# Mixer and expert block on one Trainium2 core: the second norm and the store of the result moved one group later, loads issued in the order in which tiles come free, transposed Y in another bank

## The reference, cut to what matters

```python
def reference(x, ...):                      # x: (8, 1024, 128), fp32
    x = _layernorm(x + mixer(x))            # "first norm": gives Y
    x = _layernorm(x + experts(x))          # "second norm": gives the result
    return x

def mixer(x):                               # mLSTM: up projection, causal conv, q, k, v, gates
    ...
    h = (C / norm) @ v                      # C = q k^T * exp(decay - max), causal, 4 heads
    hn = normalise(h per head)
    return ((hn * norm_w + skip * x_act) * silu(z)) @ W_down

def experts(x):                             # 16 experts of width 64, top 4 of 16, plus a shared one
    g = sigmoid(x @ gate_w.T)
    combine = top-4 of g, divided by their sum
    h = silu(x @ e_win) * (x @ e_vin) * combine
    return silu(x @ ws_in) * (x @ vs_in) @ ws_out + h @ e_wout
```

## Time and profile before

| | us |
|---|---|
| median of 3 runs | 912.57 (912.12 to 923.52) |
| the profiled execution | 916.93 |
| its span in the trace | 915.2 |
| second phase, from the first y1 to the last | 698.1 |

### The profile page before, as it was taken

How to read it: one execution, slowest core, us unless ns; L and a number is a source line. 1 busy time by engine, 2 the same in 40 slices (tenths; PEclk the granted TensorE clock), 3 DMA queues, 4 the chain that set the end, 5 groups by cost and what they waited for, 6 DMA issues and landing times.

```text
span 915.2 us, 17726 instructions
## 1 busy us (share of the span) xinstructions
PE 823.2 (90%) x5783; PEld 643.9 (70%) x5783; DVE 669.4 (73%) x1759; ACT 363.3 (40%) x621; POOL 372.1 (41%) x372
## 2 busy tenths in 40 slices
PE   6879866799999999899989999999999999999966
PEld 5646655677777777777777777777777777777754
DVE  5899944577777777777786878777867777878654
ACT  4767742224343434333333443333434343433131
POOL 5040037253536262626262626353726353534200
PEclk8999977699999999999999999999999999999979
DMA  4877734300403040404030403040304040400000
GB/s 114 258 242 271 272 116 119 115 25 24 126 23 126 24 126 23 126 23 126 23 126 23 126 23 126 23 126 23 126 23 126 23 126 23 126 23 24 1 11 12
DMA packets 53104, 81.01 MB, mean 89 GB/s; under 512 B 10176, under 2 KB 36952, under 8 KB 49112
## 3 DMA queue, kind: packets, MB, share of 16 engines
q1 hardware_dynamic: 53080, 80.68, 28.2%
HBM read 55.24 MB, written 25.43 MB: 88 GB/s over the span
## 4 chain that ended last, share of the span: by engine, by line
PE 49%; DVE 17%; issue 14%; DMA 10%; POOL 5%; SPq 3%; ACT 2%; POOLq 1%; DVEq 0%; ACTq 0%
PE bank L1402 12%; DMA max_b<-max_scratch 7%; PE bank L1372 5%; PE bank L1376 5%; PE bank L1373 5%; PE bank L1392 4%; PE bank L1345 3%; DVE st L991 3%; PE bank L1321 3%; DVE acc L839 2%; PE bank L1319 2%; DVE Y L1003 2%; PE bank L1326 2%; DMA x_in<-in_L_attn_x_dram 2%; DVE out_sb L1003 2%
## 5 line engine op out<-in xcount | busy, mean ns | idle before, releaser
L755 ACT ACTIVATE s_in<-bank 128x512 f32<-128x512 f32 x144 | 85.9, 597 | 195.9 <-PE bank L1376 195.0
L1402 PE MATMUL bank<-ewout,h 128*128 128x128 f32 x1024 | 146.5, 286 | 0.0
L1402 PEld LDWEIGHTS bank<-ewout,h 128*128 128x128 f32 x1024 | 123.9, 191 | 25.4 <-issue 25.4
L554 POOL TENSOR_TENSOR rs<-ve,half 128x4 f32<-128x4 f32 x32 | 32.6, 1019 | 267.5 <-DVE ve L999 267.5
L1103 DVE TENSOR_TENSOR h<-s_in,bank 128x512 f32<-128x512 f32 x144 | 98.1, 681 | 58.5 <-PE bank L1376 50.3
L1372 PE MATMUL bank<-yT_hi,in_hi 128*128 128x512 f32 x288 | 128.2, 445 | 6.8 <-DVE h L1103 6.8
L1376 PE MATMUL bank<-yT_lo,in_hi 128*128 128x512 f32 x288 | 115.3, 400 | 0.0
L1373 PE MATMUL bank<-yT_hi,in_lo 128*128 128x512 f32 x288 | 114.6, 398 | 0.0
L540 POOL TENSOR_TENSOR D<-a_tok,max_b 128x512 f32<-128x512 f32 x64 | 65.4, 1043 | 118.5 <-DVE max_b L911 67.9
L1107 DVE TENSOR_TENSOR h<-h,bank 128x512 f32<-128x512 f32 x128 | 87.3, 682 | 19.8 <-PE bank L1392 19.8
L952 DVE TENSOR_TENSOR state<-kept,bank 64x130 f32<-64x130 f32 x128 | 36.6, 286 | 64.8 <-POOL kept L569 34.7
(11 more groups left out here) (197 smaller groups left out, 1634.2 us busy)
## 6 DMA issues: line engine op xcount, KB each, us to landing
xact_scratch<-xact SPq DMA_DIRECT2D x16, 1024.0 KB, 4.9
max_b<-max_scratch SPq DMA_DIRECT2D x15, 1024.0 KB, 7.7
xa<-xact_scratch SPq DMA_DIRECT2D x16, 512.0 KB, 6.4
silu_z<-xact_scratch SPq DMA_DIRECT2D x16, 512.0 KB, 3.8
inter_w<-inter_scratch SPq DMA_DIRECT2D x30, 256.0 KB, 7.0
x_in<-in_L_attn_x_dram SPq DMA_DIRECT2D x16, 256.0 KB, 4.9
xt_scratch<-x_t SPq DMA_DIRECT2D x16, 256.0 KB, 4.8
xT<-xt_scratch SPq DMA_DIRECT2D x16, 256.0 KB, 8.0
```

The costliest lines, as they stand in the source:

```text
L755: act.activation(s_in[:, j % 2], bank[4][:], ACT.Silu).then_inc(silu_done, 1)
L1402: i = pe.matmul(bank[7][:, k * P:(k + 1) * P], h2[:, j % 2, k * P:(k + 1) * P], w, start=(j == k == 0), stop=(j == NJ), skip_group_check=True)
```

## The change

Four things are moved; no arithmetic is added or removed.

1. The statistics of the second norm of group f and the norm itself leave the end of `mix(f + 1)`. In `mix(g, f)` VectorE now does `ffn_statistics(f - 1)` behind slot 2 and `ffn_norm(f - 1)` behind slot 4. Only the sum z2 stays where it was.
2. GpSimd's inverse root rs2 moves with them: from behind rs1 to behind the loop over the four chunks, for group f - 1. Between rs1 and qs nothing is left.
3. SyncE stores the result of group f - 1 behind the load of xa, and then loads max_b for group g + 2 (it waits for the four subtractions of `args(g + 1)` to be done). Before, max_b for g + 1 was loaded at the start of `mix(g)`, behind the store of the group before and x_res.
4. The transposed Y goes to bank 5 and no longer to bank 7, so the waits for z2 move from `ffn_head` to the first output matmul, and waits for h1 and h2 of the group before are added.

The first two and the last two groups stand outside the hardware loop now.

```diff
             mix(0, None)
-            with eng.Fori(1, NG - 1) as g:
+            mix(1, 0)
+            with eng.Fori(2, NG - 2) as g:
                 mix(g, g - 1)
+            mix(NG - 2, NG - 3)
             mix(NG - 1, NG - 2)
             ffn(NG - 1)
...
             def mix(g, f):
-                sp.wait_ge(arg_sub, nth(g, 4, 3))
-                if not (isinstance(g, int) and g == NG - 1):
-                    load_max(g + 1)
+                if not is_last(g):
                     sp.wait_ge(val_mm[1], g + 1)
                     sp.dma_start(xT2[:], xt_d[g + 1]).then_inc(xT_in, 16)
                     sp.wait_ge(qs_done, g + 1)
...
                     load_xa(g + 1)
+                if f is not None and before(f) is not None:
+                    store(before(f))
+                if not is_last(g, 2):
+                    sp.wait_ge(arg_sub, nth(g + 1, 4, 3))
+                    load_max(g + 2)
+                if not is_last(g):
                     for p in range(NP):
                         sp.wait_ge(hs_done[p], g + 1)
                     load_z(g + 1)
-                if f is not None:
-                    store(f)
-                if not (isinstance(g, int) and g == NG - 1):
                     sp.wait_ge(y1_done, g + 1)
                     sp.dma_start(x_res[:], x_g[g + 1]).then_inc(x_res_in, 16)
...
+                if f is not None and before(f) is not None:
+                    norm_power(before(f))
                 for kp in range(2):
...
                 pool.wait_ge(ve1_done, g + 1)
                 power(rs1[:], ve1[:], rs1_done)
-                if f is not None:
-                    ffn(f)
                 if not (isinstance(g, int) and g == NG - 1):
                     weigh_queries(g + 1)
...
             def ffn_head(f):
                 act.wait_ge(yT_mm, f + 1)
-                prev2(act, z2_done, f)
-                copy(yT[:], bank[7][:]).then_inc(yT_out, 1)
-                copy(yT_hi[:], bank[7][:]).then_inc(yT_hi_done, 1)
+                copy(yT[:], bank[5][:]).then_inc(yT_out, 1)
+                copy(yT_hi[:], bank[5][:]).then_inc(yT_hi_done, 1)
...
             def mixer_norm(g):
                 dve.wait_ge(rs1_done, g + 1)
+                prev(dve, z2_done, g)
                 normalise(Y, y1, mv1, rs1, Y_done)
...
                 for j in range(NJ + 2):
                     if f is not None:
                         ffn_slot(f, j)
+                    if f is not None and before(f) is not None:
+                        if j == 2:
+                            ffn_statistics(before(f))
+                        elif j == 4:
+                            ffn_norm(before(f))
...
                 yT_low(g)
-                if f is not None:
-                    ffn_norm(f)
...
             def ffn_sum(f):
                 dve.wait_ge(o_mm, f + 1)
+                prev(dve, out_done, f)
                 dve.tensor_tensor(flat(z2), bank[7][:], flat(Y), ALU.add).then_inc(z2_done, 1)
-                dve.wait_ge(z2_done, f + 2)
+
+            def ffn_statistics(f):
+                dve.wait_ge(z2_done, f + 1)
                 statistics(f, z2, st2, mv2, ve2, st2_done, mv2_done, ve2_done)
...
             def ffn_head(f):
                 pe.wait_ge(Y_done, f + 1)
-                prev2(pe, z2_done, f)
+                prev(pe, h1_done, f, NJ + 1)
                 for k in range(NC):
-                    i = pe.transpose(bank[7][:, k * P:(k + 1) * P], Y[:, k], ident[:])
+                    i = pe.transpose(bank[5][:, k * P:(k + 1) * P], Y[:, k], ident[:])
                 i.then_inc(yT_mm, 1)
 
             def ffn_logits(f):
                 pe.wait_ge(yT_out, f + 1)
+                prev(pe, h2_done, f, NJ)
```

More of the change, by code:

```diff
@@ L323, in groups, with before, is_last @@
             mix(0, None)
-            with eng.Fori(1, NG - 1) as g:
+            mix(1, 0)
+            with eng.Fori(2, NG - 2) as g:
                 mix(g, g - 1)
+            mix(NG - 2, NG - 3)
             mix(NG - 1, NG - 2)
             ffn(NG - 1)
+        def before(f):
+            return None if isinstance(f, int) and f == 0 else f - 1
+        def is_last(g, n=1):
+            return isinstance(g, int) and g >= NG - n
         def prev(eng, s, g, per=1):
@@ L333, in prev @@
             eng.wait_ge(s, g * per)
-        def prev2(eng, s, f):
-            eng.wait_ge(s, f + 1)
         @block.sync
@@ L476, in store, with ffn @@
                 sp.dma_start(out_g[f], out_sb[:]).then_inc(out_stored, 16)
-            groups(sp, mix, store)
+            sp.wait_ge(arg_sub, 4)
+            load_max(1)
+            def ffn(f):
+                store(f - 1)
+                store(f)
+            groups(sp, mix, ffn)
             sp.wait_ge(out_stored, 16 * NG)
@@ L590, in mix, with norm_power, ffn @@
                 power(rs1[:], ve1[:], rs1_done)
-                if f is not None:
-                    ffn(f)
                 if not (isinstance(g, int) and g == NG - 1):
                     weigh_queries(g + 1)
-            def ffn(f):
+            def norm_power(f):
                 pool.wait_ge(ve2_done, f + 1)
                 power(rs2[:], ve2[:], rs2_done)
+            def ffn(f):
+                norm_power(f - 1)
+                norm_power(f)
             pool.memset(state[:], 0.0).then_inc(phase2_const, 1)
@@ L915, in _ @@
             back(2, floor_tok)
-            dve.sem_inc(z2_done, 1)
             all_tok = lambda t: t[:].rearrange("p b f k h -> p (b f) (k h)")
@@ L1041, in mix @@
                 yT_low(g)
-                if f is not None:
-                    ffn_norm(f)
             def yT_low(f):
                 dve.wait_ge(yT_hi_done, f + 1)
-                dve.tensor_tensor(yT_lo[:], bank[7][:], yT_hi[:].bitcast(F32), ALU.subtract).then_inc(yT_lo_done, 1)
+                dve.tensor_tensor(yT_lo[:], bank[5][:], yT_hi[:].bitcast(F32), ALU.subtract).then_inc(yT_lo_done, 1)
             def routing(f, part):
@@ L1128, in ffn @@
                         routing(f, 3)
+                    elif j == 2:
+                        ffn_statistics(f - 1)
+                    elif j == 4:
+                        ffn_norm(f - 1)
                 ffn_sum(f)
+                ffn_statistics(f)
                 ffn_norm(f)
@@ L1398, in ffn_out @@
                     pe.wait_ge(h1_done, nth(f, NJ + 1, 0))
+                    prev(pe, z2_done, f)
                 w = ewout[:, j - 1] if j else wsout[:]
```

## The result

| | before | after |
|---|---|---|
| median, us | 918.01 (4 runs, 912.12 to 923.52) | 983.74 (4 runs, 982.05 to 985.92) |
| profiled execution, us | 916.93 | 985.23 |
| span, us | 915.2 | 983.2 |
| group, second to fifteenth y1, 13 intervals, us | 46.32 | 51.18 |

The ratio after to before is 1.072, with a 95% interval of 1.062 to 1.081: 7% slower. The table has one run of the kernel before more than the prediction had. The ratios given there are against those runs, so the 912.57 from which the prediction started was low.

What follows compares the result with a forecast made beforehand. TensorE's work plus its waits was taken to bound each group. Two blockings gave +26.9 us and clock falls +17.4, together 44.3 on 916.93, or 961.2; the median lies 4.4 lower, so 957 us, range 930 to 988.

Steps and rivals of the forecast that it cites:

- the two blockings: GpSimd's bulk instructions block VectorE at Y behind qs and routing behind D; +26.9 us together with the clock full.
- the first case: Both blockings, with falls of the clock in some groups: 946 to 985 us, forecast 957, chance 0.47.
- the clock down nearly always: Rival: the clock falls behind both waits in most groups, 26.9 + 38 us and more, over 978; chance 0.05.
- What bounds the kernel, and what the change removes: TensorE's work plus waits set the group, 46.32 us; waits from late max_b and the norm on VectorE's path go.
- neither blocking: Rival: neither blocking comes back, a group is 44.14 us and the time 882 us; chance 0.06.
- Y behind qs: VectorE's four Y instructions wait for GpSimd, taking 3.85 us; TensorE gets Y 1.72 later, chunk 1 comes 0.92 later.
- The rule of the Trainium skill: VectorE and GpSimd share a port pair, whole instructions block; by it the sum would be some 1 us x 13 more.
- Routing behind D: Routing part 3's five small VectorE instructions each sit out a GpSimd instruction; +2.29 us from chunk 1 to next y1.
- The clock, +17.4: TensorE's new waits bring half clock in six of 13 groups, 2.9 us each; bounds 0 and 38 us.
- The moved work at nothing: Second norm's statistics behind slot 2 and norm behind slot 4 on VectorE cost 0; upper bound 14 us.
- Banks, other loads: nothing: New waits on banks 5, 6 and 7 cost 0; earlier xT2, inter_w and x_res loads bring no cost or gain.
- The last group, -1.0: No qs follows rs1 there, so Y is free 1.0 us earlier and TensorE, waiting 4.77, gains it.

Runs made afterwards that it cites:

- Early max_b with D held: Kernel before with only max_b loaded early, loop unrolled, and GpSimd starting D only after the routing weights are written: 903.42 us, 0.980 of the kernel before.
- both waits held: Changed kernel with GpSimd waiting for Y before qs and for the routing weights before D: 883.12 us, 0.960 of the kernel before.
- Y's blocking alone: Changed kernel with D held behind the routing weights and 8 unused identity matmuls before TensorE's wait for Y: 916.44 us, 0.995 of the kernel before.
- the filled waits: Changed kernel with unused identity matmuls before TensorE's waits for Y and the routing weights: 956.26 us with 12 in each, 949.26 with 8.
- the run with the spare one: Changed kernel with D held behind the routing weights and an unused inverse root between rs1 and qs on GpSimd: 885.20 us, 0.962 of the kernel before.

## Why the prediction was right, point by point

The sign, the two blockings and their places were right, and 983.74 lies in the range of 930 to 988. It lies close to the range's end, though, and the forecast of 957 was 27 us short. By the number it is still in the first case (946 to 985, falls in some groups). By what happened it is closer to the last (the clock down nearly always, over 978), which had a chance of 0.05. That the range held was in part luck. Where the 27 us are:

| us | in the sum | measured, by spans and y1 |
|---|---|---|
| first phase and first interval | 0 | +3.1 |
| 13 intervals, second to fifteenth y1 | +27.0 + 17.4 | +63.3 |
| interval to the last y1 | +0.9 | +2.2 |
| behind the last y1 | -1.0 | -0.6 |
| median against the profiled execution | -4.4 | -1.5 |

So 19 us are missing in the 13 groups, most of them in the clock's term. Of the other 8, two lie in front of the first y1, which comes anywhere from 165.6 to 176.8 us in the runs here, and three are the low median from which the prediction started.

- **What bounds the kernel, and what the change removes.** Right. Early max_b with D held gained 14 us, and the norm out of the way 1.05 us a group. With neither blocking the prediction had 44.14 a group and 882 us; measured 44.25 and 883.12. That the total agrees so well is in part luck: it started from a low median, and the first interval, which it left as it was, gave 6.7 us (50.50 to 43.78). That max_b would be issued some 20 us before a group ends was off, without effect: in the group shown it is issued at 568.15, 13 us before the end, and D never waited for it.
- **Y behind qs, 3.85 us and TensorE 1.72 later.** Right: 3.86, and the transposes of Y come 537.95 - 530.40 = 7.55 behind y1 instead of 5.64, 1.9 later. Two tenths are missing from the term: 0.1 because rs1 started 2.52 behind y1 (2.41 in the first group), the rest between the end of Y and the transposes. From 12.54 to 14.51 the prediction made 1.97 a group of it; from y1 to chunk 1 it is 12.61 with both waits held and 14.77 with Y's blocking alone, and the groups give 46.43 - 44.25 = 2.2.
- **The rule of the Trainium skill** ("SBUF — State Buffer", section "SBUF: two separate sides") that the whole instruction blocks would have added 1 us more a group. Y's 3.86 us in every group, shorter than qs, `kept` and the skip product together (2.35 + 0.62 + 1.57), is against it for the skip product. For qs and `kept` the trace agrees: the first two instructions of Y take 2.36 and 0.66 us.
- **Routing behind D, +2.29.** Right where the clock is full: 48.71 - 46.43 = 2.28, and from chunk 1 to the next y1 33.9 us with routing blocked and 31.6 without, as forecast (33.89 and 31.60). In the changed kernel itself the wait was 2.08, not 2.5, and chunk 1 to y1 33.4: some of the time that the half clock cost was given back there.
- **The sum without the clock**, 48.40 a group, measured 48.71: 0.3 short, nearly all of it in Y's term.
- **The clock, +17.4: the term that was mis-sized.** "I take a fall in six of the 13 groups" was wrong: it fell in all 13, and twice in two of them. (51.18 - 48.71) x 13 = 32 us, against 17.4; with the 0.3 a group of the line above it is 36. The price of one fall was about right: chunk 1 comes 17.74 us behind y1 instead of 14.8, 2.9 later, of which 0.5 comes back behind it. The prediction also had the place wrong. It laid the falls behind the second wait, as the longer one, from a row where 2.32 us of idling was followed by a fall and 2.07 was not. In the changed kernel the wait for Y, 2.16 us, brought the clock down each time, and the one for the weights in two groups of 13 only (there 2.50 and 2.13). The bound of a fall in each group, 38 us, was the nearer value. Nothing in the rows of the kernel before could tell six falls from 13, and the choice near the middle was a guess.
- **The moved work at nothing.** Right: the statistics fit in front of the third state update (0.3 us of idle left), and no new wait stands in slots 2 to 6.
- **Banks, other loads: nothing.** Right for the banks (1.000). The other loads and the store were not moved alone. No wait of TensorE in the changed kernel is put down to them, and with both waits held the group is within 0.1 of the sum.
- **The last group, -1.0.** Right: TensorE's wait there is 3.76 us against 4.77:

```profile
940.63 1.11 PE L1378 MATMUL bank<-ident,Y 128*128 128x128 f32 x4 [3.76 <-DVE Y L1015]
```

Open is why the clock falls at the same place in every group of the changed kernel. A wait of 2.5 brought it down in all 13 groups of one run and in two of another, so the length of a wait alone doesn't tell it. That the filled waits kept the clock up shows that TensorE's idle time has a part in it; what decides in which group it falls was not tried.

## What to carry to other kernels

Before removing a wait, ask what it holds apart. Here a late DMA and a 1 us power on GpSimd kept GpSimd's bulk instructions off the moments at which VectorE worked from SBUF to SBUF on TensorE's path; both waits looked like pure loss, and one wait in the place of each turned 7% slower into 4% faster than before. Look for such a guard in the iterations that lack it: the first and second group of the old kernel showed both costs, to within 0.3 us a group. And where a change leaves TensorE idle for about 2 us in each iteration, take a fall of the clock in every iteration as a case of its own with a fair chance. Here it came in all 13 groups of two runs, in 11 of two others and in two of a fifth.

## What the runs showed of the hardware that was not expected

- Foreseen from the earlier trace rows, and now seen in every group: VectorE's small conversions and subtractions from SBUF to SBUF each waited out one bulk instruction of GpSimd: 0.53 to 1.00 us instead of 0.20 to 0.23, the first one 0.27 or 0.69 after it had met part of one. The first two instructions of Y did the same; the third took 0.74 us beside the skip product, which ran on for 0.8 us more. GpSimd's power of 128x4 (1.0 us) doesn't hold up Y (1.11 us beside it, in all groups of the run with the spare one).
- The clock was worth as much as the wait in front of its fall: a wait of 2.16 us was followed by a loss of about 2.5.
- Filling one wait moved the fall to the next one (972.79, 1% less than unfilled); only filling both kept the clock up.
